# Another order of the operations in a pipelined stack of layers, the last items and the tail as straight lists of calls, and a token shift blended on VectorE

## The reference

```
for i in range(6):
    xn = layernorm(x, ln1_w[i], ln1_b[i])
    q, k, v = heads(xn @ wq[i]), heads(xn @ wk[i]), heads(xn @ wv[i])   # 8 heads of 16
    q = softmax(q, over the head's 16);  k = softmax(k, over the tokens)
    x = merge(q @ (k^T v)) @ wo[i] + bo[i] + x
    xn = layernorm(x, ln2_w[i], ln2_b[i])
    x = leaky_relu(xn @ w1[i]) @ w2[i] + x                               # 128 -> 512 -> 128
```

```
xr = mu_r * x + (1 - mu_r) * x_prev;  xk = mu_k * x + (1 - mu_k) * x_prev   # x_prev: one token earlier
out = sigmoid(xr Wr^T) * (relu(xk Wk^T)^2 Wv^T)
```

## Time and profile before

| | us |
|---|---|
| median of three runs | 848.62 |
| profiled execution | 846.2 |
| its span in the trace | 844.3 |
| PE busy in it | 791.0 (94%) |
| DVE busy | 662.4 (78%) |
| ACT busy | 584.7 (69%) |
| POOL busy | 462.1 (55%) |

### The profile page before, as it was taken

One profiled execution on the slowest core, in us unless ns is written; L12 is line 12 of the kernel. 1 busy time (PEld: TensorE's weight loads), 2 busy tenths in 40 slices (PEclk: granted clock), 3 DMA queues, 4 the chain that ended last, 5 costly groups with the idle time before them and its releaser, 6 DMA issues.

```text
span 844.3 us, 16194 instructions
## 1 busy us (share of the span) xinstructions
PE 791.0 (94%) x5354; PEld 687.8 (81%) x5354; DVE 662.4 (78%) x1937; ACT 584.7 (69%) x1244; POOL 462.1 (55%) x740
## 2 busy tenths in 40 slices
PE   7689999999999999999999999989999999998864
PEld 3468888999899989999899998878888887877752
DVE  4668788888788788788878787897875799999951
ACT  3466777787787777777777777778777657756353
POOL 6888556565576536544554445543454355566543
PEclk9799999999999999999999999999999999999996
DMA  9200000100000000100001000000000000000001
GB/s 258 94 0 2 1 1 1 39 1 2 1 26 14 2 2 1 38 2 1 1 2 39 1 1 1 1 1 3 1 1 1 2 1 2 2 14 26 14 14 38
DMA packets 19729, 13.70 MB, mean 16 GB/s; under 512 B 2488, under 2 KB 18495, under 8 KB 19647
## 3 DMA queue, kind: packets, MB, share of 16 engines
q1 hardware_dynamic: 19646, 12.67, 5.2%
HBM read 10.57 MB, written 2.10 MB: 15 GB/s over the span
## 4 chain that ended last, share of the span: by engine, by line
PE 76%; POOL 9%; DVE 7%; issue 4%; ACT 3%; DMA 0%; POOLq 0%; ACTq 0%; DVEq 0%
PE PS L317 68%; PE PS L327 8%; POOL XI L767 2%; ACT BIG L913 1%; POOL QB L877 1%; POOL RSTD L790 1%; POOL RSTD L797 1%; POOL RX L758 1%; ACT XR L956 1%; DVE QSM L1537 1%; DVE STATS L1273 1%; DVE STX L1258 1%; POOL R L725 1%; DVE ST L1194 0%; DVE XR L1315 0%
## 5 line engine op out<-in xcount | busy, mean ns | idle before, releaser
L317 PEld LDWEIGHTS PS<-W,HL 128*128 128x128 f32 x1536 | 194.1, 191 | 13.3 <-issue 5.3
L317 PE MATMUL PS<-W,HL 128*128 128x128 f32 x1536 | 202.0, 275 | 0.0
L969 ACT ACTIVATE HL<-PS 128x512 f32<-128x512 f32 x192 | 109.3, 593 | 14.5 <-PE PS L317 10.6
L779 POOL TENSOR_TENSOR JOIN<-STATS 128x8 f32<-128x8 f32 (+1 forms) x48 | 12.2, 254 | 159.0 <-DVE STATS L1273 159.0
L317 PE MATMUL PS<-X2H,W1L 128*128 128x512 f32 x192 | 91.6, 477 | 2.6 <-issue 2.2
L1138 ACT ACTIVATE EK<-PS,NKM 128x512 f32<-128x512 f32 x48 | 33.0, 688 | 76.7 <-DVE NKM L1498 76.7
L886 POOL TENSOR_TENSOR QB<-QB,QRC 128x512 f32<-128x512 f32 x48 | 50.9, 1061 | 56.5 <-DVE QRC L1540 56.5
L956 ACT ACTIVATE XR<-XI,RSTD 128x128 f32<-128x128 f32 x192 | 61.5, 393 | 25.4 <-POOL RSTD L797 25.3
L317 PE MATMUL PS<-X2H,W1H 128*128 128x512 f32 x192 | 76.2, 397 | 0.0
L317 PE MATMUL PS<-X2L,W1H 128*128 128x512 f32 x192 | 76.0, 396 | 0.0
L1273 DVE BATCH_NORM_STATS2 STATS<-XI 128x6 f32<-128x128 f32 x352 | 75.5, 277 | 0.1
(11 more groups left out here) (215 smaller groups left out, 2167.2 us busy)
## 6 DMA issues: line engine op xcount, KB each, us to landing
W<-in_w SPq DMA_DIRECT2D x12, 256.0 KB
X<-in_x SPq DMA_DIRECT2D x8, 256.0 KB, 4.6
out<-X SPq DMA_DIRECT2D x8, 256.0 KB, 2.3
QKV<-in_qkv SPq DMA_DIRECT2D x6, 192.0 KB, 2.8
FWD<-in_fwd SPq DMA_DIRECT2D x1, 1024.0 KB, 5.5
INV<-in_inv SPq DMA_DIRECT2D x1, 1024.0 KB, 8.1
WO<-in_wo SPq DMA_DIRECT2D x6, 64.0 KB
FWDX<-in_fwdx SPq DMA_DIRECT2D x1, 256.0 KB, 6.5
```

What stands on the lines that cost most here:

```text
L317: return nc.tensor.matmul(o, l, r, start=start, stop=stop, skip_group_check=True)
L969: nc.scalar.activation(HL[f][:, :], pH[f % 2][:, :], ACT.Prelu, alpha=LEAK).then_inc(s["hl"], 1)
```

## The change

The loop now covers items up to 43 (`layers` stops at FIRST = 44) with another order in each engine's `step`; the operations have become functions with their own waits (`keys(i)`, `attend(i)`, ...), called through `run`. What items 44 to 47 still need and the whole tail stand behind it as one straight list of calls on each engine, with the waits for a buffer's readers given by name (`hidden(44, 0, relu=3)`). The keys' and queries' three-pass products stand next to each other, and the hidden ones in pairs. The slices of the convolution kernel come three to a step over 22 steps, and its spectrum (36 products) in steps 37 to 39, in the loop. In the tail the token shift is blended on DVE before the products: `blend` makes XK and XM from the transposed sample and two copies of it that ACT scales by 1 - mu, so that key is two instructions and the gate eight. The output projection has its weights centred once, so its norm takes no mean. The norms of the tail write into XI. In the diff the four `step` functions are those of PE, POOL, ACT and DVE, in this order; behind PE's the first and last calls of its straight list stand.

```diff
-    for n in range(STEPS_IN_ALL):
-        slots = tuple((max(min(n - k, ITEMS - 1), 0) // BATCH) % 2 for k in range(4))
+    for n in range(begin, FIRST):
         layer, b = divmod(n, BATCH)
-        step(n, b, slots, layer)
+        step(n, b, layer)
...
-SLICES = {DECAY + 3 + i: 2 * i for i in range(PAIRS // 2)}
-KERNEL_OUT = DECAY + 3 + PAIRS // 2
+SLICES = {DECAY + 3 + i: 3 * i for i in range(1 + PAIRS // 3)}
+KERNEL_OUT = DECAY + 4 + PAIRS // 3
 CENTRE, CENTRE_IN = KERNEL_OUT + 2, KERNEL_OUT + 3
-SPECTRUM = {ITEMS: (0, 1, 2, 3), ITEMS + 1: (4, 5, 6, 7, 8)}
-STEPS_IN_ALL = FIRST + BATCH + 9
+SPECTRUM = {CENTRE + 4: (0, 1, 2, 3), CENTRE + 5: (4, 5, 6, 7), CENTRE + 6: (8,)}
...
+            def step(n, b, layer):
+                run(values, n - 1)
...
+                run(turn, n)
+                if n < 3:
+                    keep_busy(1)
+                run(merge, n - 1)
+                run(second, n - 3, 0)
                 if n in SLICES:
                     kernel_slice(SLICES[n] + 1)
+                run(attend, n - 1)
+                run(hidden, n - 3, 2)
+                run(keys, n)
+                run(queries, n)
+                if b == 0:
                     value_bias(layer)
+                run(hidden, n - 3, 3)
+                run(second, n - 3, 1)
+                run(second_turn, n - 2)
+                run(second, n - 3, 2)
                 centre(n)
                 for unit in SPECTRUM.get(n, ()):
                     spectrum(unit)
+                run(weights_turn, n)
+                run(second, n - 3, 3)
+                if n in SLICES:
+                    kernel_slice(SLICES[n] + 2)
+                run(context, n)
                 if n == 0:
                     keep_busy(2)
+                run(hidden, n - 2, 0)
+                run(hidden, n - 2, 1)
+                if b == 0:
                     output_bias(layer)
...
+            values(43); turn(44); merge(43); second(41, 0); attend(43); hidden(41, 2); keys(44); queries(44)
...
+            gate(5, r_sig=5); shift_turn(6, blend=6); key(5, rv=5); value(5, r_relu=6); gate(6, r_sig=6)
+            key(6, rv=6); shift_turn(7, blend=7); value(6, r_relu=7); key(7, rv=7); gate(7, r_sig=7)
+            value(7, r_relu=8)
...
+            def step(n, b, layer):
+                run(queries_scale, n - 1)
+                join(n)
+                run(second_root, n - 1)
+                run(queries_shift, n)
+                run(first_root, n + 1)
+                if n + 1 in CHUNKS:
+                    if n == DECAY:
+                        pool.wait_ge(s["la"], 1)
+                    exponents(CHUNKS[n + 1])
+                if 0 <= n < BATCH - 3:
+                    input_rstd(n + 3)
+                    input_norm(n + 3)
+                if b == 0:
+                    first_low(layer)
+                if b == 1:
+                    centre_second(layer)
...
+            def step(n, b, layer):
+                run(queries_exp, n - 1)
+                run(context_copy, n - 1)
+                run(first_scale, n)
...
+            def step(n, b, layer):
+                run(queries_reciprocal, n - 1)
+                run(second_scale, n - 2)
+                run(masked, n - 1)
+                run(queries_out, n - 1)
+                run(scaled_merge, n - 1)
+                run(stream_low, n)
+                run(first_residual, n - 1)
+                run(second_stats, n - 1)
...
+                run(keys_reciprocal, n)
+                run(second_low, n - 2)
+                run(second_residual, n - 3)
+                run(queries_sum, n)
                 if n + 3 < BATCH:
                     input_stats(n + 3)
                 if b == BATCH - 1 and layer + 1 < LAYERS:
                     centre_output(layer + 1)
-                if b == 1 and has_n:
+                if b == 1:
                     second_sums(layer)
...
             def key(v, **readers):
                 held(readers)
                 pe.wait_ge(s["blend"], v + 1)
-                mm(pY[:, :], WK1[:, :], SH[:, 1:1 + SEQ], True, False)
-                mm(pY[:, :], WK2[:, :], SH[:, 0:SEQ], False, True).then_inc(s["k2_ps"], 1)
+                mm(pY[:, :], WKT[:, :], XK[:, :]).then_inc(s["k2_ps"], 1)
...
+            def blend(v):
+
+                dve.wait_ge(s["sh_T"], v + 1)
...
+                stt(out=XK[:, :], in0=pX2[:, :], scalar=MU[:, 1:2], in1=SHK[:, 0:SEQ], op0=ALU.mult, op1=ALU.add)
+                stt(out=XM[:, :], in0=pX2[:, :], scalar=MU[:, 0:1], in1=SHR[:, 0:SEQ], op0=ALU.mult,
+                    op1=ALU.add).then_inc(s["blend"], 1)
```

More of the change, by code:

```diff
@@ L358, in _, with freed, held @@
             pe.wait_ge(s["eighth"], 1)
[L360 to L367 removed]
+            def freed(name, count):
+                if some(count):
+                    pe.wait_ge(s[name], count)
+            def held(readers):
+                for name, count in readers.items():
+                    pe.wait_ge(s[name], count)
@@ new lines, in context, with values @@
+            def context(i, **readers):
+                held(readers)
+                freed("ek", i + 1)
+                pe.wait_ge(s["ek_tm"], i + 1)
+                for j in range(TILES):
+                    last = mm(pK[:, 0:P], XR[:, j * P:(j + 1) * P], EKT[:, j * P:(j + 1) * P], j == 0, j == TILES - 1)
+                last.then_inc(s["g_ps"], 1)
+            def values(i):
+                pe.wait_ge(s["wv"], i // BATCH + 1)
+                pe.wait_ge(s["gt"], i + 1)
+                mm(pK[:, P:2 * P], WV[slot(i)][:, :], GT[:, :]).then_inc(s["c_ps"], 1)
@@ new lines, in merge, with attend @@
+            def merge(i):
+                pe.wait_ge(s["wo_c"], i // BATCH + 1)
+                pe.wait_ge(s["ct"], i + 1)
+                mm(pK[:, 2 * P:3 * P], CT[:, :], WO[slot(i)][:, :]).then_inc(s["m_ps"], 1)
+            def attend(i, **readers):
+                held(readers)
+                freed("q_fm", i + 1)
+                pe.wait_ge(s["m_ready"], i + 1)
+                pe.wait_ge(s["qs"], i + 1)
+                for j in range(TILES):
+                    last = mm(pQ[:, j * P:(j + 1) * P], QS[:, j * P:(j + 1) * P], MM[:, :])
+                last.then_inc(s["out_ps"], 1)
@@ new lines, in _ @@
+            context(44); hidden(42, 0); hidden(42, 1); values(44); turn(45); merge(44); second(42, 0); attend(44)
+            hidden(42, 2); keys(45); queries(45); hidden(42, 3); second(42, 1); second_turn(43); second(42, 2)
+            weights_turn(45); second(42, 3); context(45); hidden(43, 0); hidden(43, 1); values(45); turn(46)
+            merge(45); second(43, 0); attend(45); hidden(43, 2); keys(46); spiking_turn(0, x2h=44); queries(46)
+            hidden(43, 3); second(43, 1); second_turn(44, in_T=1); second(43, 2); weights_turn(46)
@@ new lines, in _ @@
+            spiking_first(0, 0, hl=175); spiking_first(0, 1, hl=176); spiking_first(0, 2, relu=1)
+            spiking_first(0, 3, relu=2); second(43, 3); context(46); hidden(44, 0, relu=3); spiking_second(0, 0)
+            spiking_second(0, 1); hidden(44, 1, relu=4); spiking_second(0, 2); values(46); spiking_second(0, 3)
+            turn(47); spiking_turn(1, x2h=45); merge(46); second(44, 0); attend(46); spiking_first(1, 0, hl=177)
+            spiking_first(1, 1, hl=178); spiking_first(1, 2, relu=5); spiking_first(1, 3, relu=6)
@@ L769, in input_norm, with join_parts @@
                 last.then_inc(s["xi_init"], 1)
-            def join(first, end, turn):
+            def join_parts(first, end, turn):
                 def part(i):
@@ new lines, in keys_exp, with queries_copy @@
+            def keys_exp(i):
+                act.wait_ge(s["kmax"], i + 1)
+                if some(i):
+                    act.wait_ge(s["ekT_ps"], i)
+                    act.wait_ge(s["k_rec"], i)
+                nc.scalar.activation(EK[:, :], pK[:, :], ACT.Exp, bias=NKM[:, 0:1], accum_out=KSM[:, 0:1]).then_inc(s["ek"], 1)
+            def queries_copy(i):
+                act.wait_ge(s["q_ps"], i + 1)
+                if some(i):
+                    act.wait_ge(s["q_blk"], i)
+                copy(QF[:, :], pQ[:, :]).then_inc(s["q_fm"], 1)
@@ L1144, in step @@
[L1144 to L1155 removed]
+                run(rectified, n - 3, 2)
@@ L1162, in step @@
[L1162 to L1172 removed]
+                run(weights_copy, n)
@@ L1332, in late_weights, with queries_reciprocal, masked @@
+            def queries_reciprocal(i):
+                dve.wait_ge(s["q_sum"], i + 1)
+                if some(i):
+                    dve.wait_ge(s["q_nrm"], i)
+                nc.vector.reciprocal(QRC[:, :], QSM[:, :]).then_inc(s["q_rec"], 1)
+            def masked(i):
+                dve.wait_ge(s["c_ps"], i + 1)
+                if some(i):
+                    dve.wait_ge(s["m_ps"], i)
+                tt(CT[:, :], pK[:, P:2 * P], HMASK[:, :], ALU.mult).then_inc(s["ct"], 1)
             def late_weights(n):
```

907 lines of the change are left out of this document (407 added, 500 removed).

## The result

The changed kernel took 903.41 us (median of 4 runs, 900.42 to 904.97), beside 848.12 for the kernel before on the same chip (846.89 to 849.23, 4 runs): a ratio of 1.0656, 95% interval 1.0637 to 1.0676. It is slower by 55 us, more than three times the 15.5 that were forecast. The side was right, the size and the range (846 to 876) were not.

What follows compares the result with a forecast made beforehand. Pool was taken to bound the fill, PE the middle, DVE 740 to 800 us, then a chain. 846.2 + 17.5 + 15 - 2 + 4 - 19 = 861.7, plus 2.4 for the median: 864 us, range 846 to 876.

Steps and rivals of the forecast that it cites:

- The fill, +17.5: Start to keys of item 5: queries' scaling behind the input norm leaves POOL waiting, steps of 15.15 us: +17.5 us.
- the 4.0 forecast for the chain: Fill: POOL waits from the scaling's end through sum, attend, residual and stats, with handovers, 4.0 us a step.
- The clock: Fill: 6 to 12 us more PE work at the lower clock would cost 3 to 6 us, not summed.
- New weights, +15: Steps at n = 8, 16, 24, 32, 40: early BM copy and weight work delay PE, +15 us, bounds 0 and 22.
- WO's 0.8: New weights, b=7: WO's centring on DVE ahead of the queries' reciprocal costs 0.8 us a layer, bounds 0 and 1.3.
- Steady steps, -2: Loop steps: 11.5 us without slices, 12.05 with three, against 11.87 before; in all -2 us (0 to -5).
- The spectrum's +4: Items 37 to 39: the spectrum's 36 matmuls move from the end to where PE is full, +4 us.
- The end, -19: Turn of item 44 to the end: straight list, DVE bound, then a chain of 30; sum 272.7 us, -19.
- C: Rival: the fill costs nothing, as PE's slack lets later steps catch up; 846.6 us, no change, chance 0.11.
- D: Rival: faster, the straight list fills holes, end at its bound (-25), fill only +10; 835 us, chance 0.12.
- E: Rival: the end gives nothing, blends on a full DVE eat what the list brings; 883 us, chance 0.06.
- B: Rival: slower still, PE at the lower clock in each fill step and in the end; 872 to 876 us, chance 0.15.

Runs made afterwards that it cites:

- experiment 2: Changed kernel with DVE's statistics of input sample n+3 moved ahead, right behind the statistics of item n-1; POOL's order as changed: 888.32 us.
- experiment 4: Changed kernel with six thrown-away products of a constant tile on PE ahead of attend in steps 1 to 5: 892.44 us.
- experiment 5: Changed kernel with ACT's copy of the bias BM put behind the scaling of the next stream, as before: 886.92 us.
- experiment 6: Changed kernel with fill scaling and reciprocal ahead of input work, BM's copy late, W1, W2, WO work behind the queries' scaling or reciprocal: 848.07 us.
- experiment 7: Changed kernel with its loop up to item 43 in the order of the kernel before, three slices, straight lists and blend kept: 848.82 us.
- experiment 9: As experiment 7, but two slices a step, with the late weights' work and the spectrum as calls in the straight lists: 846.61 us.
- experiment 11: Kernel before with the blended token shift alone, blends on DVE, three ACT copies: 858.42 us.
- experiment 8: As experiment 7, but with the token shift of the kernel before, without blends on DVE: 852.05 us.
- experiment 10: As experiment 6, but two slices a step, late weights' work and spectrum moved to the straight lists: 851.14 us.

## Why the prediction was wrong

The span grew by 54.0 us, where the sum had 15.5. Of the 38.5 between them the fill has 16.5, the new weights 11.3, the end 7.7, the steady steps 2.2 and the spectrum 0.8.

**The fill, +17.5, measured +34.0: the step that failed.** The prediction wrote: "Without the scaling ahead of it that norm could start 1.1 earlier, but DVE must have the statistics of sample 3 first; I take 0.3." It named the very dependence and used it for the first turn only; the turn of 15.15 us then let the input norm follow the first root at once. In the traces the turn is 20.0. POOL's rows account for the difference of 4.8: 2.6 for the statistics (experiment 2: 2.8 a turn), 1.2 ahead of the subtraction, and 0.9 in the first wait, which is 4.91 and not 4.0. The last two are PE's lower rate: attend lies in the first wait, keys and queries in the second, and in experiment 4, with PE near its full rate (0.96), they are 3.99 and 0.19. So the 4.0 forecast for the chain was right for a PE that doesn't slow down. The first turn, where the dependence was used, came out by luck: keys 1 were forecast at 34.45 and started at 34.38, but the scaling ended at 31.6 and not 32.4, and the keys followed it by 2.8 and not 2.05.

**The clock, "in the range, not in the sum", 3 to 6 us.** The mechanism was right; the size in the fill was 8 us (keys of item 5 at 105.43 in place of 113.57, the granted clock at 0.96 in place of 0.79), and it came back in the steps with new weights, where the prediction didn't look for it, with 1.1 us in three of five. The rule of the Trainium skill weighed there (TensorE: Matmul & The Clock Gate, Part 1: throttled by default, released by activity) is borne out by experiment 4: more products, a higher granted clock, less time. The clock's cost belonged into the sum, as each turn had an idle time of several us.

**New weights, +15, measured +26.3.** The place and mechanism were right: BM ahead of the exponential, GT and XR; an idle of 1.7 us against 2.2 forecast. BM's part came to 14.6 us of the 26.3 (experiment 5), 2.9 a layer against 2.2, for the clock comes on top of the idle time. The W1, W2 and WO work ahead of the queries came to 4.8, which experiment 6 takes away beyond experiment 5 (this row of the table goes from 211.3 to 196.5 and 191.7); that is 1.0 a layer, where 2.2 were forecast. WO's 0.8 is not to be found: the steps behind keys 7, 15, 23 and 31 are 12.75 to 12.77 us, and 12.64 to 12.88 in experiment 6. Another 4.7 are there in the old order too (experiment 7, 189.7 against 185.0): the third slice, which the forecast has under the steady steps, and the late weights of steps 33 and 34, which had no term. Without these 4.7 the row is 21.6, close to the forecast's 22 before 6.5 were deducted for old waits; but it is made of other parts, so that is partly luck. That the old waits stayed is a reading of this sum, which no run shows.

**Steady steps, -2, measured +0.2; slices.** 12.03 with three slices (12.05 forecast) was right, 11.8 to 11.9 without (11.5 forecast) was not. The spectrum's +4 is found in keys 35 to 40 (+4.8).

**The end, -19, with +4 booked elsewhere; measured -11.3.** From the turn of item 44 (617.76) to the last output (864.07) it took 246.3 us, forecast 242.7. The last chain took 34.2, forecast 30: DVE's last gated product came 24.5 us behind the output, before it was 20.8; the mean granted clock in this chain was 0.68, against 0.82 in the last stretch before. And the deeper reading was wrong: the gain is not the lists' (experiment 9), it is work moved forward, where it costs the same. That DVE is the bound there, so that "what PE saves is worth nothing", fits the loop's order (experiment 11), but not the lists, for which it was said (experiment 8).

**The rivals.** C and D were far off. E's 883 lies nearest to 903, but by an end that gives nothing, and the end gave 11.3 us. B (872 to 876, slower still by the clock in the fill and in the end) has a part of the mechanism, but not the statistics.

**The signs.** Keys(2) started at 53.46 (49 to 52 forecast), keys(5) at 113.57 (95 to 100), PE was busy 21.70 of the 40.5 us from 13 to 53.5 (24) and POOL waited 4.91 ahead of the join (about 4). The idle time in the step of item 8 came in two parts, and the larger one was ended by GT and not by XR. From the turn of item 44 it took 280.5 us (265 to 280).

Still open: why moving the late work back costs the mended order 8 us and gives it only 6 (experiment 10), what makes the clock fall after some idle times and not after others that are as long, and what the shortest last chain would be.

## What to carry to other kernels

When an order changes, follow the moved operation once around: list what each instruction in the turn waits for, and include the independent ones that stand behind a dependent one in an in-order list (here the statistics of an input sample behind a sum of the running item). If the walk returns to its start, the sum of the whole circle is the step, however idle each engine looks. And when a stretch gets shorter, check first that its work wasn't moved out: here 10 of 11 us had been.

## What the runs showed of the hardware

After idle times of 1.14 and 0.57 us in a stretch where PE was busy 1.78 of 3.50 us, the granted clock was 0.67 over the next 4.5 us in the step of item 8, and 1.00 after the same two idle times in the step of item 16; with the idle gone (experiment 5) it was 1.00. Eight products of attend took 2.05 us behind an idle time of 5.62 us, and 1.13 behind 5.32 us of thrown-away products (experiment 4). Six such products ahead of each attend made the kernel 9.6 us faster, by a ratio of 1.0543 against 1.0656.
